# Reordering VectorE's step in a latent-attention stage: a tile's maxima first, then the next queries and keys

## The reference, cut to what matters

```python
def attention(x, Wq, Wk, Wv, Wo):
    xr = rope(x)
    Q, K, V = xr @ Wq, xr @ Wk, xr @ Wv      # 16 heads of 16; keys and values shared by 4 heads
    scores = einsum('bghsd,bgtd->bghst', Q, K) / sqrt(16)
    mask = triu(full((S, S), -1e9), k=1)
    attn = softmax(scores + mask, axis=-1)
    return einsum('bghst,bgtd->bghsd', attn, V) @ Wo
h = x + attention(rms_norm(x, norm1_w), Wq, Wk, Wv, Wo)
h = h + moe(rms_norm(h, norm2_w), ...)       # router needs every tile of h
```

## Time and profile before

| | |
|---|---|
| median of 3 runs | 1037.44 us (1036.21 to 1040.33) |
| the profiled execution | 1034.94 us |
| its span, from first to last instruction | 1033.1 us |
| PE busy | 786.5 us (76%) |
| PE weight loads busy | 571.0 us (55%) |
| DVE busy | 519.6 us (50%) |
| ACT busy | 440.8 us (43%) |
| POOL busy | 437.2 us (42%) |
| mean granted TensorE clock | 0.871 of full speed |

### The profile page before, as it was taken

The page is one execution under the profiler, slowest core; times in us unless marked ns, Lnnn a source line. Parts: engine busy times, 40 slices in busy tenths (PEclk is TensorE's granted clock), DMA queues, the critical chain, the costliest instruction groups (busy, mean ns, idle before and its releaser), DMA issues.

```text
span 1033.1 us, 21352 instructions
## 1 busy us (share of the span) xinstructions
PE 786.5 (76%) x7200; PEld 571.0 (55%) x7200; DVE 519.6 (50%) x1397; ACT 440.8 (43%) x1523; POOL 437.2 (42%) x637
## 2 busy tenths in 40 slices
PE   2788987699779566999975626765555999999980
PEld 1676766588644235777754415654432566666660
DVE  3466766467733344667665765666231333223323
ACT  1667667246514225777751023766102333333320
POOL 4566654434468768687722334354341000000005
PEclk9999999889879888999996756886556999999995
DMA  8322214723331545454410003122292065152004
GB/s 285 137 67 79 70 53 143 240 73 95 123 124 54 190 133 170 147 172 136 155 51 0 0 0 122 43 83 97 92 391 77 27 223 179 49 189 93 16 23 122
DMA packets 66199, 116.83 MB, mean 113 GB/s; under 512 B 6576, under 2 KB 22704, under 8 KB 65456
## 3 DMA queue, kind: packets, MB, share of 16 engines
q1 hardware_dynamic: 57936, 105.25, 30.3%
q10 hardware_dynamic: 6624, 6.03, 1.8%
q0 software_dynamic: 1536, 4.20, 1.3%
HBM read 81.11 MB, written 34.34 MB: 112 GB/s over the span
## 4 chain that ended last, share of the span: by engine, by line
PE 48%; DVE 15%; POOL 13%; ACT 9%; issue 8%; DMA 4%; ACTq 0%; SPq 0%; DVEq 0%; POOLq 0%; another core or an unknown queue 0%
ACT probs L1208 6%; PE ps L622 4%; PE ps L1046 4%; PE ps L1047 4%; PE ps L1048 4%; PE ps L638 3%; PE ps L1069 2%; PE ps L1071 2%; PE ps L1070 2%; PE ps L1058 2%; PE ps L520 2%; DVE probs L1710 2%; POOL probs L1454 2%; PE ps L662 2%; PE ps L521 2%
## 5 line engine op out<-in xcount | busy, mean ns | idle before, releaser
L1393 POOL TENSOR_TENSOR piece_out<-piece_in,piece_out 128x512 f16<-128x512 f32 x96 | 116.6, 1215 | 7.7
L1609 POOL DMA_INDIRECT pt<-y_rows,neg x16 | 15.4, 960 | 233.4 <-DMA y_rows<-vbuf 228.8
L2133 DVE TENSOR_TENSOR probs<-ps,ctx_t 128x512 f32<-128x512 f32 x46 | 29.6, 686 | 154.0 <-PE ps L1048 154.0
L622 PE MATMUL ps<-pack_const,probs 128*128 128x128 f32 x512 | 74.3, 278 | 17.0 <-issue 13.1
L1358 POOL TENSOR_TENSOR var<-mv,half 128x1 f32<-128x1 f32 x48 | 9.6, 199 | 179.4 <-DVE mv L1625 107.7
L622 PEld LDWEIGHTS ps<-pack_const,probs 128*128 128x128 f32 x512 | 55.9, 140 | 37.7 <-issue 26.0
L1392 POOL CAST piece_out<-piece_in 128x512 f16<-128x512 f32 x96 | 62.2, 648 | 23.0 <-DMA piece_in<-in_w 22.1
L1046 PE MATMUL ps<-arena,qbuf 128*128 x184 | 70.7, 384 | 0.0
L1047 PE MATMUL ps<-arena,qbuf 128*128 x184 | 70.5, 383 | 0.0
L1048 PE MATMUL ps<-arena,qbuf 128*128 x184 | 70.3, 382 | 0.0
L1158 ACT ACTIVATE probs<-ps,mx 128x256 f32<-128x256 f32 x128 | 59.2, 487 | 15.6 <-DVE mx L1721 15.6
(11 more groups left out here) (285 smaller groups left out, 2178.5 us busy)
## 6 DMA issues: line engine op xcount, KB each, us to landing
piece_in<-in_w SPq DMA_DIRECT2D x96, 256.0 KB, 2.8
w_parts<-piece_out SPq DMA_DIRECT2D x96, 256.0 KB, 2.1
arena<-w_parts SPq DMA_DIRECT2D x8, 3072.0 KB, 12.7
ctx_t<-in_ctx SPq DMA_DIRECT2D x32, 256.0 KB, 2.8
x_rows<-piece_out SPq DMA_DIRECT2D x1, 2944.0 KB, 17.3
qbuf<-x_rows ACTq DMA_DIRECT2D x23, 128.0 KB, 2.4
y_rows<-vbuf ACTq DMA_DIRECT2D x23, 128.0 KB, 1.9
arena<-in_xa SPq DMA_DIRECT2D x2, 1282.0 KB, 7.8
```

What stands on the lines that cost most here:

```text
L622: last = pe.transpose(AB[:, o:o + P], pr[:, 2 * c + n, kt * P:(kt + 1) * P], ident)
L1393: pool.tensor_tensor(both[:, PIECE:], src, both[:, 0:PIECE], ALU.subtract).then_inc(piece_split, 1)
```

## The change

It reorders stage la (`st == "la"`) on two engines; stage sa keeps its order. No instruction is added or taken away.

- On DVE a step begins with `sum_values` and `row_maxima` of tile k-1 and `copy_queries_and_keys` of tile k. After them come `gather_outputs` (k-3), `scale_probs` (k-2), the residual (k-3) and `xn` (k-3).
- On PE `project(k)` stands right behind `score(k-1)`, and `join_heads(k-3)` ahead of `turn_probs(k-2)`.
- Two waits on AB follow the new order: `project(i)` waits for the copied probabilities of tile i-3 in place of i-2, and `turn_probs(i)` for the copied queries and keys of tile i+2 (count i+3) in place of i+1.

```diff
-                    hold(pe, g["pt_copied"], 2 * (i - 2) + 1)
+                    hold(pe, g["pt_copied"], 2 * (i - (2 if st == "sa" else 3)) + 1)
...
-                    hold(pe, g["qk_copied"], at_most(i + 2, TILES))
+                    hold(pe, g["qk_copied"], at_most(i + (2 if st == "sa" else 3), TILES))
...
                     if live(k, 1, TILES):
                         score(k - 1)
+                    if live(k, 0, TILES) and st == "la":
+                        project(k)
                     if live(k, 4, TILES):
                         turn(k - 4)
+                    if live(k, 3, TILES) and st == "la":
+                        join_heads(k - 3)
                     if live(k, 2, TILES):
                         turn_probs(k - 2)
...
                 for k in range(INNER_STEPS):
+                    if st == "la":
+                        if live(k, 1, TILES):
+                            sum_values(k - 1)
+                            row_maxima(k - 1, (k - 1) % 2)
+                        if live(k, 0, TILES):
+                            copy_queries_and_keys(k)
                     if live(k, 3, TILES):
                         gather_outputs(k - 3)
                     if live(k, 2, TILES):
                         scale_probs(k - 2, k % 2)
-                    if live(k, 1, TILES):
+                    if live(k, 1, TILES) and st == "sa":
                         sum_values(k - 1)
                         row_maxima(k - 1, (k - 1) % 2)
...
-                    if live(k, 0, TILES):
+                    if live(k, 0, TILES) and st == "sa":
                         copy_queries_and_keys(k)
```

More of the change, by code:

```diff
@@ L860, in inner @@
                         score(k - 1)
+                    if live(k, 0, TILES) and st == "la":
+                        project(k)
                     if live(k, 4, TILES):
                         turn(k - 4)
+                    if live(k, 3, TILES) and st == "la":
+                        join_heads(k - 3)
                     if live(k, 2, TILES):
                         turn_probs(k - 2)
-                    if live(k, 3, TILES):
+                    if live(k, 3, TILES) and st == "sa":
                         join_heads(k - 3)
-                    if live(k, 0, TILES):
+                    if live(k, 0, TILES) and st == "sa":
                         project(k)
```

## The result

| | before | changed |
|---|---|---|
| median of 4 runs | 1036.83 us (1036.19 to 1040.33) | 1063.17 us (1061.59 to 1063.89) |
| span of the profiled execution | 1033.1 us | 1059.7 us |
| mean granted TensorE clock | 0.871 | 0.865 |

What follows compares the result with a forecast made beforehand. The prediction took a 12.00 us loop over VectorE, ScalarE and POOL in stage la as the bound. 1034.94 + 25 = 1060 us, 1062.4 from the median, gave 1061; range 1048 to 1068 for 8 in 10.

Steps and rivals of the forecast that it cites:

- The loop of the kernel before: Stage la: VectorE gathering to maxima 5.84 us, 0.04, then exponentials, square, POOL and `xn` 6.12; 12.00 us a step.
- Exponentials behind the copies: ScalarE, stage la: exponentials of tile k-1 cannot start at their maxima, but wait for tile k-2's scaled, turned, copied probabilities.
- The step: Stage la, one step at the lower clock: 16.7 to 16.8 us in place of 12.00, 4.8 more.
- The sum over the stage: Stage la's added time at the lower clock: 1.0 + 2.9 + 4.3 + 19.2 = 27.4 us; 25 taken.
- The early steps: First steps of stage la: exponentials delayed by 1.0, then 2.9 more, then 4.3 more us at the lower clock.
- TensorE's clock: Transposes in stage la: 1.97 us at the lower clock, 1.10 at the upper; lower expected after longer idling, chance 0.62.
- The sum at the lower clock: Stage la with slow transposes and projection on TensorE: 27.4 us more in all.
- The slack of the other loop: Loop through the next scores on TensorE: mixing, values and scores end near 13.6, 3 us ahead of the next step.
- still slower: Rival, stage la: lower clock also delays queries and keys or mixing, up to 1 us a step; +33, 1069; chance 0.06.
- Nothing absorbed behind the stage: After stage la: a later end moves the first expert matmul and all that follows by as much.
- faster: Rival, stage la: exponentials start at the end of the maxima; step 9.3 us, -13 us, 1023; chance 0.04.
- my two sums: Stage la's added time: 17.3 us at the upper TensorE clock, 27.4 at the lower.

Runs made afterwards that it cites:

- turning-first kernel: The changed kernel with the probabilities turned ahead of the output projection again on TensorE in stage la: 1065.73 us, 1.0275 of the kernel before.

## Why the prediction was right, point by point

**The loop of the kernel before** was read rightly. Taking POOL's two instructions out of it moved the step from 12.00 to 10.97 us, and the only kernels that were faster than before are those that shortened this loop.

**Exponentials behind the copies.** Shown twice: the changed kernel's ScalarE has no idle time between second copy and exponentials while the maxima wait 6.9 us, and reversing just these two gives back 11 us.

**The step.** 16.7 to 16.8 us were forecast; 16.1 to 16.5 came (16.86 in the first). The terms one by one, forecast and chain: values to maxima 3.2 and 3.20; query and key copies 1.3 and 1.23; gathering to the end of the projection, 2.55 after 1.2, and 2.50 after 1.18; turning and copies 2.60 and, at the lower clock, 2.55; to the next step 6.12 and 6.00. The sum was a little long, since most terms were and neighbours overlap.

**The sum over the stage** was 27.4 at the lower clock, and 25 was given. Exponentials of tiles 1, 2, 3 and 7 started at 646.14, 661.33, 677.01 and about 741.2. The whole stage began 0.2 us later, so they are 1.1, 6.2, 10.9 and 27.1 late, where 1.0, 3.9, 8.2 and 27.4 had been worked out. The end agrees by two errors that cancel. The early steps cost 2.7 us more: I had taken mixing, values and scores from rows at full clock, about 3.0 us, and here they ran at the lower one, 1.11, 2.07 and 1.99 in the timeline of TensorE:

```profile
646.30 1.11 PE L807 MATMUL ps<-pt,vbuf 64*32 64x128 f32 x32 [0.69 <-ACT pt L1202]
647.34 2.07 PE L754 MATMUL ps<-arena,xt_all 128*128 128x256 f32 x4
649.34 1.99 PE L767 MATMUL ps<-kbuf,qbuf 32*128 32x64 f32 x32
```

The later four steps, from exponentials to exponentials, cost 16.2 and not 19.2. Three were 0.3, 0.7 and 0.3 us shorter than counted, and the last 1.6, since it has no query and key copies (there is no ninth tile), which I had overlooked. So that the sum comes so near is partly luck; the length of the steady step is not.

**TensorE's clock.** The sum at the lower clock was the right one. Of the eight groups of transposes seven took 1.87 us or more and one, at 707.50, took 1.49. But the reason given, that TensorE would idle longer ahead of the turning, is not what decided it: in the kernel before seven of the eight took 1.97 already, at a granted clock of 0.69 from 672 to 740 us against 0.68 after. The choice was right and its reason not shown. The Trainium skill's rule (What's actually happening, in "TensorE: Matmul & The Clock Gate"), that throttled is the default and activity releases it, agrees with both experiments that added matmuls: 0.67 to 0.88 and 0.62 to 0.91 over the same 56 us.

**The slack of the other loop** was put at 3 us, from rows at full clock. In the changed kernel it was smaller: mixing to scores took 5.0 us there and ended at 698.67, 0.9 ahead of the next step at 699.60; one step later, at the upper clock, it was 3.2 ahead. This step of the prediction was weak, and the wrong forecast for the turning-first kernel came from the same place. The rival "still slower" named this mechanism with a chance of 0.06.

**Nothing absorbed behind the stage**: right, 26.7 us at the first expert matmul, 26.6 in the span.

**The rival "faster"** decided at one point, the end of the second copy. It ended at 693.58 - 683.13 = 10.45 us into the step, where 10.6 had been forecast and 3.2 would have been needed. The statement on ScalarE's queue that the prediction takes from the Trainium skill stands in the page named there, but in its section "Architectural detail: the array is 16× 32×32, not 1× 128×128".

What stays open: how much of the changed kernel's loss is the clock's. The added matmuls gave back 5 us, but the clock still fell in some steps, so the full difference of 10 us between my two sums was neither shown nor excluded. Nor was TensorE's new order run by itself in the kernel before, so its share of the 7.4 us is read from the chain only.

## What to carry to other kernels

Follow a moved instruction to the in-order list of the engine that consumes it: an earlier result is worth nothing while something that was made later stands ahead of its consumer there. When a pipeline's step is one loop over several engines, write down the loop and what lies beside it; an edit that puts things from beside it into it costs their full length in every step. And price the second-longest loop at the lower TensorE clock too, for it may take over.

## What the runs showed of the hardware that was not expected

A tiny VectorE instruction can wait for POOL without any semaphore. The scaling of 128x16 maxima took 0.17 us as a rule and 1.00 when a POOL instruction of 1.15 us was under way, ending 0.03 us after it. This happened in six tiles, and without the instruction the stage was 5.5 us shorter. It is not so for every instruction: in the changed kernel the copy of the values out of PSUM at 683.13 took its usual 0.41 us while a POOL instruction ran from 683.00 to 684.22.

"SBUF — State Buffer" (SBUF: two separate sides) in the Trainium skill says that VectorE and GpSimd share one pair of ports under an exclusive lock, held for a whole instruction by whichever starts first; on VectorE's side it names only operations in a two-port mode or with two inputs from SBUF. The rows agree in that the later one waits to the end of the other. In which mode the scaling ran no run here shows, so the lock as the cause is not shown.

And work that nobody needs can make a kernel faster: ten matmuls a step, about 4.5 us of TensorE, took 0.45% and 0.75% off two kernels whose loop ran through TensorE at its lower clock. The first figure is near the noise, the second clear of it.
